# Second attention of a two-block network: the rounding and the rest of q one round later, the output projection cut into three groups of tiles, the output weights rounded later

## The chip, the core and the metric

The kernel runs on one core of one Trainium2 chip. The metric is the device time of one execution in microseconds (us), as the median of several runs. Before the change three runs took 1021.14, 1026.47 and 1027.76 us.

## What is computed

Two transformer blocks on x of shape (2, 512, 512), each one an attention and a feed-forward part with adaptive layer norm. The change touches only the attention of the second block, a latent attention with 32 heads:

```python
q = (rmsnorm(h @ w_qa) @ w_qb)            # per head: 128 plain + 64 rotary
k_c, k_rope = split(h @ w_kva)            # 64 + 64, k_c normalized
k_nope, v = split(k_c @ w_kvb)            # per head
scores = q_head @ k_head.T * 192 ** -0.5
attn = softmax(scores)
out = concat_heads(attn @ v) @ w_o
x = x + ga * out
```

The kernel has folded the key and value weights of each head into the q weights and the output weights before this stage starts. What is left per head is a q of 128 rows (64 latent, 64 rotary), its scores against one shared key, a softmax, a context of 64 latent columns, and an output projection. All matrix products are done in a rounded format with a correction: an operand f is kept as `hi` (rounded, made by ScalarE) and `lo` = f - `hi` (the rest, made by VectorE or GpSimd), and a product is hi*hi + hi*lo + lo*hi.

## The kernel before, in words

**Units, couples, rounds, steps.** A unit u is one head of one batch (64 units). A couple j is two heads (32 couples). Each unit has four rounds, one for each 128 of its 512 query rows, so there are 256 rounds s. All five engines run through the same loop `for s in range(STEPS)`, each with its own list of work for step s; 8 steps are the period of a couple. Below, r stands for s mod 8. Each engine works its own list strictly in the order in which it is written; semaphores tie the lists together.

**The work of one round s.** TensorE: `scores(s)`, three matmuls of 128x128 by 128x512 into one of two PSUM banks (L1289 to L1291), which wait until the exponential of round s-2 has read that bank. VectorE: `row_max(s)` (L1351) reads the scores, then `row_inv(s-1)` (L1358). ScalarE: `exps(s)` (L1429) with the maximum as bias. GpSimd: `normalize(s-1)` (L1488) for three rounds of four, ScalarE for the fourth (L1444). VectorE: `turn(s-3)` (L1366), the 32x32 transposes. When four rounds are turned, 16 DMAs move the unit's blocks (12 on SyncE's queue, 4 on ScalarE's, L1254).

**q of a coming unit.** TensorE projects unit s/4+2 at s mod 4 = 0 (`project`, five matmuls, L1275 to L1279). VectorE turns it by the rotary angles in three operations: part 0 (L1341, in the step with s mod 4 = 1) and parts 1 and 2 (L1343, L1346, s mod 4 = 2). They write `qu` and `qf`, which are parts of the buffer that the profile calls stage_a. GpSimd adds the two, `q_sum` (L1479), at s mod 4 = 3. ScalarE rounds the sum to `q_hi` (`q_round`, L1423) and GpSimd makes `q_lo` (`q_rest`, L1483), both at s mod 4 = 0. There is one `qf` and one `qu`: part 0 of a unit waits for `q_sum` of the unit before it (`ge(dve, qsum, u)`), and part 2 for its `q_lo` (`ge(dve, qlo_done, u)`).

**Context and output projection of couple j.** They run at the steps s = 8(j+2) + r. TensorE: `context` at r = 1 and r = 3, eight matmuls each (L1302). ScalarE: `cT_hi` at r = 3 (L1461). VectorE: `cT_lo` at r = 4 (L1402). The output weights of the couple are rounded by ScalarE to `b_hi` (L1418) and by GpSimd to `b_lo` (L1474), both at r = 0. TensorE: `project_out` of tiles 0 and 1 at r = 5 and tiles 2 and 3 at r = 7, three matmuls a tile (L1316 to L1318), accumulated in four PSUM banks over 16 couples. The weights of a coming couple's q are rounded at r = 5 (`w_hi` L1414, `w_lo` L1469), and once at s = 0.

**The order inside a step** is that of the code. GpSimd's list in a step is: `normalize`, `q_rest`, `weights`, `out_weights`, `q_sum`, where each of them is due. ScalarE's is: `exps`, `q_round`, its share of the normalizing, its DMAs, `weights`, `out_weights`, `cT_hi`. TensorE's is: `scores`, `project`, `context`, `project_out`.

**Ends of a batch.** When the 16 couples of a batch are accumulated, VectorE multiplies the four banks by the gate, adds them to x and takes statistics (`evict`, `stats_of`; L1372, L1376, L148), in step 144 for the first batch and in the last step for the second.

Of the kernel before, what the change touches and what calls it, by code (L numbers as in the profile page):

```python
# [35 lines left out]
HP = NH // 2  # L36
UNITS = 2 * NH
COUPLES = NH
# [36 lines left out]
def megakernel(nc, a, out):  # L75
# [3 lines left out]
    with ExitStack() as whole:  # L79
# [872 lines left out]
        with ExitStack() as ph:  # L952
# [263 lines left out]
            TURN_LAG = 3  # L1216
            MOVE_LAG = TPB + TURN_LAG
            PV_AT = {1: (0, 1), 3: (2, 3)}
            OUT_AT = {5: (0, 1), 7: (2, 3)}
            ROUNDS = TPB * UNITS  # L1220
            STEPS = 8 * (COUPLES + 2) + 1

            def ge(eng, s_, v):
                if v > 0:
                    eng.wait_ge(s_, v)

            def placed(at, s):

                j, r = s // 8 - 2, s % 8
                return (j, at[r]) if r in at and 0 <= j < COUPLES else None  # L1230

            def norm_ready(eng, s):

# [23 lines left out]
            with nc.Block() as block:  # L1257
# [75 lines left out]
                @block.vector  # L1333
                def _(dve):
                    def rotate(u, part):

                        lo, hi = slice(KVR, KVR + 32), slice(KVR + 32, P)
                        if part == 0:
                            dve.wait_ge(q_ps, u + 1)
                            ge(dve, qsum, u)  # L1340
                            dve.tensor_tensor(qu[lo, :], q_bank[hi, :], sinq[hi, :], ALU.mult).then_inc(qrot, 1)  # L1341
                        elif part == 1:
                            dve.tensor_tensor(qu[hi, :], q_bank[lo, :], sinq[lo, :], ALU.mult).then_inc(qrot, 1)  # L1343
                        else:
                            ge(dve, qlo_done, u)
                            dve.tensor_tensor(qf[:, :], q_bank[:, :], cosq[:, :], ALU.mult).then_inc(qrot, 1)  # L1346

                    def row_max(s):
                        dve.wait_ge(s_ps, s + 1)
                        ge(dve, exp_done, s - RING + 1)  # L1350
                        dve.tensor_reduce(nmax[:, s % RING:s % RING + 1], s_bank[s % 2][:, :], AX.X, ALU.max,  # L1351
                                          negate=True).then_inc(max_done, 1)

                    def row_inv(s):
                        dve.wait_ge(exp_done, s + 1)
                        if s >= RING:
                            norm_ready(dve, s - RING)
                        dve.reciprocal(rinv[:, s % RING:s % RING + 1], rsum[:, s % RING:s % RING + 1]).then_inc(rinv_done, 1)  # L1358

                    def turn(s):  # L1360

                        u, st = s // TPB, s % TPB
                        norm_ready(dve, s)
                        if st == 0 and u >= T_SLOTS:
                            pT_ready(dve, u - T_SLOTS)
                        dve.transpose(blk[:, u % T_SLOTS, :, :, 32 * st:32 * st + 32].rearrange("p j k q -> p k j q"),  # L1366
                                      prob[s % RING]).then_inc(blk_done, 1)

                    def evict(b):
                        for n in range(TPB):  # L1370
                            dve.wait_ge(o_ps, 2 * HP * (b + 1) - 1 + n // 2)
                            dve.tensor_tensor(o_bank[n][:, :], o_bank[n][:, :], gate[:, 0, b, :], ALU.mult).then_inc(og_done, 1)  # L1372
                        for n in range(TPB):
                            i = TPB * b + n
                            dve.wait_ge(og_done, i + 1)
                            dve.tensor_tensor(x[:, i, :], o_bank[n][:, :], x[:, i, :], ALU.add).then_inc(x3_done, 1)  # L1376

                    def stats_of(b):
                        for t in range(TPB * b, TPB * (b + 1)):
                            dve.wait_ge(x3_done, t + 1)  # L1380
                            tile_stats(dve, t)

                    dve.wait_ge(acc_set, 1)
                    for u in (0, 1):
                        for part in range(3):
                            rotate(u, part)
                    for s in range(STEPS):
                        if s < ROUNDS:
                            row_max(s)
                        if 1 <= s <= ROUNDS:  # L1390
                            row_inv(s - 1)
                        if s % TPB == 1 and s // TPB + 2 < UNITS:
                            rotate(s // TPB + 2, 0)
                        if s % TPB == 2 and s // TPB + 2 < UNITS:
                            rotate(s // TPB + 2, 1)
                            rotate(s // TPB + 2, 2)
                        if TURN_LAG <= s < ROUNDS + TURN_LAG:
                            turn(s - TURN_LAG)
                        if s % 8 == 4 and 0 <= s // 8 - 2 < COUPLES:
                            j = s // 8 - 2  # L1400
                            dve.wait_ge(chi_done, j + 1)
                            dve.tensor_tensor(by_block(cT_lo[:, :]), ct_bank[:, :].rearrange("p (g t q) -> p g t q", g=QD, t=TPB),  # L1402
                                              by_block(cT_hi[:, :].bitcast(F32)), ALU.subtract).then_inc(clo_done, 1)
                        for b in range(B):
                            if s == 8 * (HP * (b + 1) + 2):
                                evict(b)
                                stats_of(b)

                @block.scalar
                def _(act):  # L1410
# [3 lines left out]
                        act.activation(w_hi[:, :, :, :], wq_all[:, 2 * p:2 * p + 2, :, :], ACT.Copy).then_inc(whi_done, 1)  # L1414

                    def out_weights(j):
                        ge(act, o_ps, 2 * j)
                        act.activation(b_hi[:, :], wb_all[:, j % HP, :], ACT.Copy).then_inc(bhi_done, 1)  # L1418

                    def q_round(u):  # L1420
# [14 lines left out]
                    for s in range(STEPS):  # L1435
                        u, st = s // TPB, s % TPB
                        if s < ROUNDS:
                            exps(s)
                        if st == 0 and u + 1 < UNITS:
                            q_round(u + 1)  # L1440
                        if st == (ACT_NORM + 2) % TPB and 1 <= u <= UNITS:
                            n = s - 2
                            act.wait_ge(rinv_done, n + 1)
                            act.activation(prob[n % RING], prob[n % RING], ACT.Copy,  # L1444
                                           scale=rinv[:, n % RING:n % RING + 1]).then_inc(norm_act, 1)
                        if 0 <= (s - MOVE_LAG) // TPB < UNITS:
                            m, jj = (s - MOVE_LAG) // TPB, (s - MOVE_LAG) % TPB
                            if jj == 0:
                                move_ready(act, m)
                            move(act, m, QD - 1, jj).then_inc(pT_in[m % P_SLOTS], 16)  # L1450
                        if s == 0:
                            weights(1)
                        if s % 8 == 5 and s // 8 + 2 < COUPLES:
                            weights(s // 8 + 2)
                        if s % 8 == 0 and 0 <= s // 8 - 2 < COUPLES:
                            out_weights(s // 8 - 2)
                        if s % 8 == 3 and 0 <= s // 8 - 2 < COUPLES:
                            j = s // 8 - 2
                            act.wait_ge(pv_ps, 2 * (j + 1))
                            ge(act, o_ps, 2 * j)  # L1460
                            act.activation(by_block(cT_hi[:, :]), ct_bank[:, :].rearrange("p (g t q) -> p g t q", g=QD, t=TPB),  # L1461
                                           ACT.Copy).then_inc(chi_done, 1)

                @block.gpsimd
                def _(pool):
# [30 lines left out]
                    for s in range(STEPS):  # L1496
                        u, st = s // TPB, s % TPB
                        if 1 <= s <= ROUNDS and (s - 1) % TPB != ACT_NORM:
                            normalize(s - 1)
                        if st == 0 and u + 1 < UNITS:  # L1500
                            q_rest(u + 1)
                        if s == 0:
                            weights(1)
                        if s % 8 == 5 and s // 8 + 2 < COUPLES:
                            weights(s // 8 + 2)
                        if s % 8 == 0 and 0 <= s // 8 - 2 < COUPLES:
                            out_weights(s // 8 - 2)
                        if st == 3 and u + 2 < UNITS:
                            q_sum(u + 2)
# [186 lines left out]
```

## Time and profile before

| | |
|---|---|
| median of three runs | 1026.47 us |
| the profiled execution, its time | 1023.77 us |
| its span, first to last instruction | 1021.9 us |
| mean granted TensorE clock | 0.934 |
| the stage that the change touches | from 392.1 us (first row maximum) to 952.5 us (last output projection) |

Busy time over the whole span: TensorE 849.0 us (83%), VectorE 764.2 (75%), ScalarE 535.6 (52%), GpSimd 520.7 (51%). A row of the profile gives an instruction's start, its duration, and in square brackets how long its engine had been idle before it and which instruction released it. An instruction's duration reaches into the next one's on VectorE and ScalarE, and much further on TensorE, so the cost of an instruction to its engine is read from the distance between starts.

### The profile page before, as it was taken

How to read it: one execution, taken by the hardware profiler on the slowest of the kernel's cores; microseconds unless marked ns; L12 is line 12 of the kernel's file. 1: busy time of each engine (PE TensorE's matmuls, PEld its weight loads, DVE VectorE, ACT ScalarE, POOL GpSimd, SP SyncE). 2: the span in 40 equal slices, each digit the busy share in tenths (PEclk: the TensorE clock that was granted, in tenths of full speed). 3: DMA queues.
4: the chain of work that ended last, by engine and by line, in shares of the span. 5: the costliest groups of instructions: out<-in, count | busy, mean ns of one | idle time of the engine just before them, and what ended most of it. 6: DMA issues, size and time to landing. Idle time of an engine off the chain costs nothing. (4 is left out here: it accounts for less than half of the span.)

```text
span 1021.9 us, 15116 instructions
## 1 busy us (share of the span) xinstructions
PE 849.0 (83%) x4552; PEld 563.1 (55%) x4552; DVE 764.2 (75%) x1588; ACT 535.6 (52%) x1142; POOL 520.7 (51%) x449
## 2 busy tenths in 40 slices
PE   5678886599978965799999999997999999985476
PEld 1667675477767743355555555564555555643145
DVE  1759998745535525999999999999999999982453
ACT  2267874623213743665666666564666665662143
POOL 2034342012110004888888888886888888872013
PEclk9979998599987986999999999998999999998779
DMA  9430000700023770455555555553555555555101
GB/s 328 159 129 2 1 2 1 276 23 1 1 82 126 246 227 0 111 132 126 130 130 129 128 132 131 126 131 93 129 128 132 128 130 129 127 130 118 56 11 72
DMA packets 73105, 112.29 MB, mean 110 GB/s; under 512 B 18816, under 2 KB 23936, under 8 KB 72768
## 3 DMA queue, kind: packets, MB, share of 16 engines
q1 hardware_dynamic: 60736, 94.54, 33.8%
q10 hardware_dynamic: 12288, 16.79, 6.9%
q8 instruction: 36, 0.59, 0.2%
q14 instruction: 45, 0.37, 0.1%
HBM read 42.06 MB, written 2.10 MB: 43 GB/s over the span
## 5 line engine op out<-in xcount | busy, mean ns | idle before, releaser
L1351 DVE TENSOR_REDUCE nmax<-bank 128x1 f32<-128x512 f32 x256 | 171.7, 671 | 36.1 <-PE bank L1291 35.9
L1429 ACT ACTIVATE prob<-bank,nmax 128x512 f32<-128x512 f32 x172 | 118.2, 687 | 132.9 <-DVE nmax L1351 132.1
L1488 POOL TENSOR_TENSOR prob<-prob,rinv 128x512 f32<-128x512 f32 x129 | 133.5, 1042 | 42.7 <-DVE rinv L1358 42.7
L1289 PE MATMUL bank<-xk_hi,q_hi 128*128 128x512 f32 x256 | 114.2, 446 | 28.0 <-ACT prob L1429 20.8
L1366 DVE STREAM_TRANSPOSE blk<-prob 128x512 f32<-128x512 f32 x172 | 120.0, 698 | 1.7 <-ACT prob L1444 0.4
L1289 PEld LDWEIGHTS bank<-xk_hi,q_hi 128*128 128x128 f32 x256 | 48.2, 188 | 108.8 <-issue 53.0
L1483 POOL TENSOR_TENSOR q_lo<-stage_a,q_hi 128x512 fp32r<-128x512 f32 x64 | 82.6, 1291 | 47.8 <-ACT q_hi L1423 47.8
L1290 PE MATMUL bank<-xk_lo,q_hi 128*128 128x512 f32 x256 | 101.5, 396 | 0.0
L1291 PE MATMUL bank<-xk_hi,q_lo 128*128 128x512 f32 x256 | 100.9, 394 | 0.0
L1429 ACT ACTIVATE stage_a<-bank,nmax 128x512 f32<-128x512 f32 x84 | 57.7, 687 | 56.4 <-DVE nmax L1351 56.0
L1479 POOL TENSOR_TENSOR stage_a<-stage_a 128x512 f32<-128x512 f32 x64 | 82.0, 1282 | 6.3 <-DVE stage_a L1346 6.3
L204 ACT ACTIVATE n_f<-bank,mod 128x128 f32<-128x128 f32 x128 | 48.2, 463 | 50.4 <-PE bank L195 49.2
L1316 PE MATMUL bank<-b_hi,cT_hi 128*128 128x512 f32 x128 | 54.0, 422 | 22.2 <-DVE cT_lo L1402 22.2
L1488 POOL TENSOR_TENSOR stage_a<-stage_a,rinv 128x512 f32<-128x512 f32 x63 | 65.2, 1041 | 13.6 <-DVE rinv L1358 13.6
L1302 PE MATMUL bank<-raw_e,c_all 128*64 128x512 f32 x256 | 63.2, 617 | 5.5 <-DMA raw_e<-blk 5.5
L1302 PE MATMUL bank<-pT,c_all 128*64 128x512 f32 x256 | 64.2, 625 | 3.6 <-DMA pT<-blk 3.6
L1366 DVE STREAM_TRANSPOSE blk<-stage_a 128x512 f32<-128x512 f32 x84 | 58.6, 697 | 0.6
L794 POOL TENSOR_TENSOR f_g<-f_sum,gate 128x512 f32<-128x512 f32 x8 | 10.2, 1271 | 95.4 <-DVE f_sum L870 95.4
L1423 ACT ACTIVATE q_hi<-stage_a 128x512 fp32r<-128x512 f32 x64 | 40.4, 631 | 31.4 <-POOL stage_a L1479 31.4
L1341 DVE TENSOR_TENSOR stage_a<-bank,stage_a 32x512 f32<-32x512 f32 x64 | 44.5, 695 | 14.4 <-PE bank L1279 12.3
L1291 PEld LDWEIGHTS bank<-xk_hi,q_lo 128*128 128x128 f32 x256 | 48.5, 190 | 11.3
L214 DVE TENSOR_TENSOR n_h_lo<-n_f,n_h_hi 128x512 fp32r<-128x512 f32 x24 | 16.6, 692 | 46.8 <-ACT n_h_hi L210 46.8
(217 smaller groups left out, 2135.6 us busy)
## 6 DMA issues: line engine op xcount, KB each, us to landing
pT<-blk SPq DMA_DIRECT2D x384, 64.0 KB, 2.0
raw_e<-blk SPq DMA_DIRECT2D x384, 64.0 KB, 2.0
wmod<-in_wmod SPq DMA_DIRECT2D x12, 1024.0 KB, 12.0
raw_e<-in_wo SPq DMA_DIRECT2D x8, 1024.0 KB, 6.4
pT<-blk ACTq DMA_DIRECT2D x128, 64.0 KB, 2.1
raw_e<-blk ACTq DMA_DIRECT2D x128, 64.0 KB, 2.0
wqn<-in_wqn SPq DMA_DIRECT2D x8, 512.0 KB, 4.0
stage_a<-in_wqkv SPq DMA_DIRECT2D x4, 768.0 KB, 8.9
```

Of the source, the lines that this page charges most:

```text
L204: a_ = act.activation(self.f[:, c, :], pT[:, c * P:(c + 1) * P], ACT.Identity, bias=mod3[:, self.shift + c, b:b + 1], scale=mod3[:, self.s ...
L1289: pe.matmul(sbk, q_hi[:, u % 2, q], xk_hi[:, 2, ks], start=True, stop=False)
L1290: pe.matmul(sbk, q_hi[:, u % 2, q], xk_lo[:, 1, ks], start=False, stop=False)
L1291: pe.matmul(sbk, q_lo[:, u % 2, q], xk_hi[:, 2, ks], start=False, stop=True).then_inc(s_ps, 1)
L1302: mm = pe.matmul(ct_bank[e * KVR:(e + 1) * KVR, :], c_all[:, b * TPB + kt, :], pT[(2 * j + e) % P_SLOTS][:, :, kt * P:(kt + 1) * P], start ...
L1316: pe.matmul(o_bank[n][:, :], cT_hi[:, ts], b_hi[:, :], start=(p == 0), stop=False)
L1351: dve.tensor_reduce(nmax[:, s % RING:s % RING + 1], s_bank[s % 2][:, :], AX.X, ALU.max, negate=True).then_inc(max_done, 1)
L1366: dve.transpose(blk[:, u % T_SLOTS, :, :, 32 * st:32 * st + 32].rearrange("p j k q -> p k j q"), prob[s % RING]).then_inc(blk_done, 1)
L1429: act.activation(prob[s % RING], s_bank[s % 2][:, :], ACT.Exp, bias=nmax[:, s % RING:s % RING + 1], accum_out=rsum[:, s % RING:s % RING + ...
L1479: pool.tensor_tensor(qf[:, :], qf[:, :], qu[:, :], ALU.add).then_inc(qsum, 1)
L1483: pool.tensor_tensor(q_lo[:, u % 2, :], qf[:, :], q_hi[:, u % 2, :].bitcast(F32), ALU.subtract).then_inc(qlo_done, 1)
L1488: pool.tensor_tensor(prob[s % RING], prob[s % RING], bc(rinv[:, s % RING:s % RING + 1], [P, S]), ALU.mult).then_inc(norm_pool, 1)
```

## The change

- `q_round` on ScalarE and `q_rest` on GpSimd move from the step with s mod 4 = 0 to the step with s mod 4 = 1, behind the exponential (ScalarE) or the normalizing (GpSimd) of that step.
- `project_out` is called three times a couple in place of twice: tiles 0 and 1 at r = 6, tile 2 at r = 7, and tile 3 at r = 10, which is r = 2 of the next couple's period. The semaphore `o_ps` therefore counts 3 a couple, and the waits on it are changed to match.
- `out_weights` on both engines moves from r = 0 to r = 3. On ScalarE it stands ahead of `cT_hi`, on GpSimd ahead of `q_sum`.
- `evict` and the statistics of a batch move three steps later, and the loop has four steps more.
- `placed` is rewritten so that it can look past the end of a period.

```diff
-            OUT_AT = {5: (0, 1), 7: (2, 3)}
+            OUT_AT = {6: (0, 1), 7: (2,), 10: (3,)}
-            STEPS = 8 * (COUPLES + 2) + 1
+            STEPS = 8 * (COUPLES + 2) + 5
             def placed(at, s):
-                j, r = s // 8 - 2, s % 8
-                return (j, at[r]) if r in at and 0 <= j < COUPLES else None
+                for r, parts in at.items():
+                    j = (s - r) // 8 - 2
+                    if (s - r) % 8 == 0 and 0 <= j < COUPLES:
+                        return j, parts
+                return None
                     def evict(b):
                         for n in range(TPB):
-                            dve.wait_ge(o_ps, 2 * HP * (b + 1) - 1 + n // 2)
+                            dve.wait_ge(o_ps, 3 * HP * (b + 1) - 2 + max(n - 1, 0))
...
-                            if s == 8 * (HP * (b + 1) + 2):
+                            if s == 8 * (HP * (b + 1) + 2) + 3:
                                 evict(b)
...
# ScalarE
                     def out_weights(j):
-                        ge(act, o_ps, 2 * j)
+                        ge(act, o_ps, 3 * j)
...
-                        if st == 0 and u + 1 < UNITS:
+                        if st == 1 and u + 1 < UNITS:
                             q_round(u + 1)
...
-                        if s % 8 == 0 and 0 <= s // 8 - 2 < COUPLES:
+                        if s % 8 == 3 and 0 <= s // 8 - 2 < COUPLES:
                             out_weights(s // 8 - 2)
                         if s % 8 == 3 and 0 <= s // 8 - 2 < COUPLES:
                             j = s // 8 - 2
                             act.wait_ge(pv_ps, 2 * (j + 1))
-                            ge(act, o_ps, 2 * j)
+                            ge(act, o_ps, 3 * j)
...
# GpSimd
-                        if st == 0 and u + 1 < UNITS:
+                        if st == 1 and u + 1 < UNITS:
                             q_rest(u + 1)
...
-                        if s % 8 == 0 and 0 <= s // 8 - 2 < COUPLES:
+                        if s % 8 == 3 and 0 <= s // 8 - 2 < COUPLES:
                             out_weights(s // 8 - 2)
                         if st == 3 and u + 2 < UNITS:
                             q_sum(u + 2)
```

## Rows read from the trace of the kernel before

**Rows 1.** Windows: stretch, length, busy of PE, PEld, DVE, ACT, POOL; clock; DMA

```profile
520.00:610.00 90.00, 84.05 (x341) 51.50 (x343) 84.09 (x172) 55.54 (x125) 74.81 (x67) 1.00 0.56 130
```

**Rows 2.** Waits, 400 to 940 us: who for whom, total, times, longest

```profile
DVE nmax L1351 <- PE bank L1291: 35.5, 62, 7.5
```

**Rows 3.** VectorE's timeline over one couple, from r = 2 on

```profile
718.09 0.69 DVE L1351 TENSOR_REDUCE nmax<-bank 128x1 f32<-128x512 f32 x1 [0.53 <-PE bank L1291]
...
720.84 0.65 DVE L1351 TENSOR_REDUCE nmax<-bank 128x1 f32<-128x512 f32 x1
...
723.34 0.65 DVE L1402 TENSOR_TENSOR cT_lo<-bank,cT_hi 128x512 fp32r<-128x512 f32 x1
723.91 0.67 DVE L1351 TENSOR_REDUCE nmax<-bank 128x1 f32<-128x512 f32 x1
...
724.68 0.69 DVE L1341 TENSOR_TENSOR stage_a<-bank,stage_a 32x512 f32<-32x512 f32 x1
...
726.42 0.69 DVE L1351 TENSOR_REDUCE nmax<-bank 128x1 f32<-128x512 f32 x1 [0.29 <-PE bank L1291]
...
729.16 0.65 DVE L1351 TENSOR_REDUCE nmax<-bank 128x1 f32<-128x512 f32 x1
...
731.68 0.69 DVE L1351 TENSOR_REDUCE nmax<-bank 128x1 f32<-128x512 f32 x1
```

**Rows 4.** ScalarE and GpSimd in the same couple, r = 3 to 5

```profile
721.52 0.69 ACT L1429 ACTIVATE stage_a<-bank,nmax 128x512 f32<-128x512 f32 x1 [1.93 <-DVE nmax L1351]
722.20 0.60 ACT L1461 ACTIVATE cT_hi<-bank 128x512 fp32r<-128x512 f32 x1
722.63 1.28 POOL L1479 TENSOR_TENSOR stage_a<-stage_a 128x512 f32<-128x512 f32 x1
723.95 0.63 ACT L1423 ACTIVATE q_hi<-stage_a 128x512 fp32r<-128x512 f32 x1 [0.40 <-POOL stage_a L1479]
...
724.66 1.30 POOL L1483 TENSOR_TENSOR q_lo<-stage_a,q_hi 128x512 fp32r<-128x512 f32 x1 [0.74 <-ACT q_hi L1423]
```

**Rows 5.** b_hi and b_lo, and the normalizing behind them

```profile
716.51 0.63 ACT L1418 ACTIVATE b_hi<-wb_all 128x512 fp32r<-128x512 f32 x1
...
717.88 1.28 POOL L1474 TENSOR_TENSOR b_lo<-wb_all,b_hi 128x512 fp32r<-128x512 f32 x1
719.12 2.04 POOL L1488 TENSOR_TENSOR prob<-prob,rinv 128x512 f32<-128x512 f32 x2
```

**Rows 6.** TensorE's timeline: output projection and scores at r = 5 and 6

```profile
724.04 0.50 PE L1316 MATMUL bank<-b_hi,cT_hi 128*128 128x512 f32 x1 [0.62 <-DVE cT_lo L1402]
...
725.99 0.39 PE L1291 MATMUL bank<-xk_hi,q_lo 128*128 128x512 f32 x1
```

**Rows 7.** From the maximum of r = 7 to that of r = 2

```profile
729.85 0.69 ACT L1429 ACTIVATE prob<-bank,nmax 128x512 f32<-128x512 f32 x1 [1.93 <-DVE nmax L1351]
730.68 0.50 PE L1289 MATMUL bank<-xk_hi,q_hi 128*128 128x512 f32 x1 [0.40 <-ACT prob L1429]
731.57 1.94 PE L1302 MATMUL bank<-pT,c_all 128*64 128x512 f32 x8
...
734.44 0.69 DVE L1351 TENSOR_REDUCE nmax<-bank 128x1 f32<-128x512 f32 x1 [0.53 <-PE bank L1291]
```

**Rows 8.** The stage's start: weights, and what waits for them

```profile
394.17 1.27 POOL L1483 TENSOR_TENSOR q_lo<-stage_a,q_hi 128x512 fp32r<-128x512 f32 x1 [1.12 <-ACT q_hi L1423]
395.39 1.26 POOL L1469 TENSOR_TENSOR w_lo<-wq_all,w_hi 128x512 fp32r<-128x512 f32 x1
396.70 0.79 PE L1275 MATMUL bank<-xk_hi,w_hi 128*128 128x512 f32 x1 [4.67 <-POOL w_lo L1469]
```

**Rows 9.** VectorE around the end of the first batch (s = 144 and 145)

```profile
690.61 0.65 DVE L1351 TENSOR_REDUCE nmax<-bank 128x1 f32<-128x512 f32 x1
...
698.99 0.68 DVE L1351 TENSOR_REDUCE nmax<-bank 128x1 f32<-128x512 f32 x1
```

**Rows 10.** The stage's last context

```profile
942.92 5.10 PE L1302 MATMUL bank<-raw_e,c_all 128*64 128x512 f32 x16 [5.54 <-DMA raw_e<-blk]
```

## The prediction, made blind

> **What bounds the kernel now.** I read the windows first, to see which engine is full in the stretch that the change touches. VectorE is busy for 84.09 of 90 us there and the clock is at its full 1.00 [rows 1]. TensorE's 84.05 is a sum of overlapping records; by distances between starts, eight context matmuls take 1.87 us (start to the scores behind them), 0.23 each, and a couple's 62 matmuls (24 scores, 10 of q, 16 context, 12 output) some 14.5 us. So the pace is VectorE's, and the list of waits says what it still waits for: TensorE's scores, 62 times, 35.5 us [rows 2]. VectorE's timeline over a couple shows where. A couple takes 16.35 us (718.09 to 734.44, r = 2 to r = 2), and 62 waits over some thirty couples are two a couple: 0.53 us at r = 2, 0.29 at r = 6 [rows 3, 7]. All else is its own work, 15.5 us. A change that alters neither the work nor these waits moves nothing; the most to be won is 0.8 us a couple.
>
> The wait at r = 6. TensorE's output projection stands ahead of `scores` of r = 6 and waits for `cT_lo`; it starts at 724.04, and the last score matmul starts at 725.99, 0.43 us before the maximum [rows 3, 6]. The exponential on which those scores also depend had started at 722.77 (`cT_hi` at 722.20 plus 0.57) and was no obstacle.
>
> The wait at r = 2. It hangs on a chain that starts at VectorE itself: maximum of r = 7 at 729.16, exponential 729.85, scores of r = 1 730.68, eight context matmuls 731.57, scores of r = 2, maximum 734.44: 5.28 us, of which VectorE could have done its own steps in 4.75 [rows 3, 7].
>
> **The output projection in three parts.** No matmul is added. With tiles 0 and 1 behind the scores of r = 6, these no longer wait for `cT_lo`, and the 0.29 us go. Tiles 0 and 1 then fill the time in which scores of r = 7 wait for their exponential anyway. Tile 3 (three matmuls, 0.7 us) now lies between the scores of r = 2 and r = 3. The scores of r = 2 are ahead of it, so the wait of 0.53 stays. Behind it the scores of r = 4 come later, by at most 0.7 us. The earlier exponential of r = 1 (next part) gives part of that back, and I put what is left at 0 to 0.16 us at r = 4, which is no term of its own, for the chain below starts at r = 3 and passes it by.
>
> **q one round later.** At r = 1 and r = 5 the exponential is no longer queued behind `q_hi`. But VectorE paces ScalarE; an earlier exponential is worth something only if TensorE was waiting on it in front of a late score, which is so neither at r = 2 nor at r = 6. `q_lo` comes later: its readers are part 2 of the rotation and the scores of the next unit. With `q_hi` 0.68 behind the exponential and `q_lo` 0.71 behind that [rows 4], `q_lo` is done 3.4 us behind the step's maximum, and part 2 is reached 3.7 us behind it at the earliest (the step's 2.25 without its wait, and 1.5). Zero, with a cover of 0.3; where it is gone, VectorE waits for the difference.
>
> **The output weights later: the step that decides.** `b_hi` on ScalarE now stands behind the exponential of r = 3 and ahead of `cT_hi`; `b_lo` on GpSimd stands ahead of `q_sum`. Queued behind `b_lo` is `q_sum`, and for `q_sum` waits VectorE's part 0 at r = 5, which overwrites `qu`. Count from the maximum of r = 3 (720.84). Now: exponential at +0.68, `cT_hi` +1.36, `q_sum` +1.79 to +3.07, `cT_lo` +2.50, maximum of r = 5 +3.07, part 0 +3.84, maximum of r = 6 +5.58 [rows 3, 4]. After: `b_hi` takes the place of `cT_hi` at +1.36. `b_lo` starts 0.71 later as `q_lo` does behind `q_hi` [rows 4], at +2.07. The next GpSimd instruction starts 1.24 to 1.27 behind it [rows 5]: `q_sum` at +3.33, done at +4.61. Part 0 can start at about +4.65, where it was ready at +3.84: a new wait of 0.8 us. From part 0 to the next maximum are 726.42 - 0.29 - 724.68 = 1.45 us, so the maximum of r = 6 is at +6.10 in place of +5.58: **0.52 us more a couple**, with the old wait at r = 6 already taken off. `cT_hi` comes 0.6 later, `cT_lo` could start at +2.56 instead of +2.50, and that lies inside the new wait. So does the 0.16 of tile 3.
>
> No row of before has VectorE waiting for `q_sum` here, so the handover is bounded: 0.04 us as ScalarE's (722.63 + 1.28 to 723.95) [rows 4] up to 0.1. The five terms are each good to 0.02. I take 0.52 and keep 0.42 to 0.6.
>
> At r = 7 nothing is put ahead of `q_sum`. GpSimd's list is refilled there by `w_lo` and two normalizings that come 1.3 us later than now, and by my count it has 0.5 us to spare before the value that it needs at r = 7.
>
> **How often.** `b_lo` with a part 0 two steps behind it occurs at s = 19, 27, ... 243: 29 times. Once, at s = 147, the batch's end covers it. 28 x 0.52 = 14.6 us (28 x 0.42 = 11.8).
>
> **Once each.** The batch's end costs 7.1 us of VectorE's own work (690.61 to 698.99, less a step of 1.25) [rows 9]. At r = 0 it hid the wait of r = 2 and left the 0.29 of r = 6; at r = 3 it hides the new one of r = 5 and leaves the 0.53 of r = 2: +0.2. Start: `w_lo` at s = 0 no longer stands behind a `q_lo` (394.17 to 395.39), and the projection that TensorE waits 4.67 us for starts 1.2 us sooner [rows 8]; the `q_lo` that is pushed back is then wanted by part 2 two steps on, so I take -1.0. End: tile 3 of couple 30 falls between the halves of the last context, which had waited 5.54 us for its DMA [rows 10]: 0.7 us more, up to 1.4 at half the clock; +1.0. The DMAs: SyncE's queue and ScalarE's four are moved past nothing that they wait for. Sum: 14.6 + 0.2 - 1.0 + 1.0 = **+14.8 us**, on the profiled execution's 1023.77: 1038.6. The median is 2.7 above that execution and would give 1041.3; the three runs spread over 6.6, so I stay by the profiled one and say 1039.
>
> **A rule against the change.** The granted clock is 1.00 in this stage although the matmuls come in groups with gaps [rows 1]. The Trainium skill (TensorE: Matmul & The Clock Gate, "A second HAM failure mode: psum-queue depth-cycling") tells of a kernel in which small idle times between groups of matmuls made the clock swing between its two levels. The gap that the new wait makes on TensorE is under 1.5 us, no more than now. If the clock did fall to 1.2 GHz, 62 matmuls would take 29 us in place of 14.5, some 12.7 us over the present 16.35 a couple; one couple in four would be +90 us. By that rule the kernel would be slower by that; I give it 0.02.
>
> **The rivals.**
> - *The hidden one, on the faster side.* The wait for scores at r = 6 goes and `q_sum` is in time: -0.29 x 28 - 1.0 = -9.1 us, 1014.7 on the profiled execution. It is decided at one point: `q_sum` must end before VectorE is ready for part 0, +3.84. That needs 0.8 us off a chain of exponential, `b_hi`, `b_lo` and `q_sum`, each of which has a row. Against it speaks all of rows 4 and 5; for it only that GpSimd's order may not bind as I read it. 0.06.
> - *The trade.* `q_sum` is late, but part is given back (a wait at r = 2 that shrinks, a shorter end): -3 to +8, say +4, 1028. For it: both are waits of one engine on another. Against it: the chain of r = 2 starts at VectorE's own maximum and moves along. 0.15.
> - *Two waits.* Tile 3 on TensorE or the late `w_lo` on GpSimd pushes a second reader, the maximum of r = 4 or part 0 at r = 1, 0.3 to 0.5 us more a couple: +23 to +28, 1049. For it: covers of 0.2 to 0.5 us. 0.12.
>
> **How the numbers follow.** Forecast 0.65, trade 0.15, two waits 0.12, hidden 0.06, clock 0.02. The range 1027 to 1049 takes in the forecast with 0.42 to 0.6, the upper half of the trade and the lower half of the two waits. About 1%, 10 us, is what runs of this kernel can tell from no change. Slower by over 1%: 0.14 and most of the forecast, 0.57, 0.71. Within 1%: the trade, 0.08 of the forecast and most of the hidden one, 0.25. Faster by over 1%: 0.04.
>
> **What would show it.** VectorE waits 0.7 to 0.8 us for GpSimd's `q_sum` ahead of part 0 at r = 5, 28 times; the waits for scores fall from 62 to about 31 and keep 0.53 each; a couple takes 16.9 us; `b_lo` follows `b_hi` at once, with `q_sum` right behind. I am wrong if part 0 at r = 5 has no wait, if a couple takes under 16.3 us or over 17.3, or if the clock leaves 1.00.

## The result, and the profile after

The changed kernel takes 1042.80 us (median of 4 runs, 1041.84 to 1045.10), beside 1025.62 for the kernel before (4 runs): a ratio of 1.0177, 95% interval 1.0138 to 1.0216. It is **slower by 1.8%**, 17 us. The forecast was 1039, range 1027 to 1049, and slower by over 1% with a chance of 0.71. The profiled execution took 1041.84 us with a span of 1040.0, clock 0.932; the one before had 1023.77, 1021.9 and 0.934.

The list of waits from 400 to 960 us, read as in [rows 2]:

```profile
DVE nmax L1354 <- PE bank L1294: 21.1, 35, 1.4
DVE stage_a L1344 <- POOL stage_a L1482: 20.2, 28, 1.0
POOL b_lo L1477 <- ACT b_hi L1421: 15.6, 31, 8.6
```

The waits for scores fell from 62 to 35, and their 35.5 us to 21.1. The two totals are not quite alike: that of before holds one wait of 7.5 us at the stage's start (ended at 400.25), and its counterpart of 6.5 us ended at 397.03, ahead of this window. Without it, 61 waits of 28.0 us became 35 of 21.1. In the place of those that went, VectorE waits 28 times, 20.2 us, 0.72 each, for `q_sum`: a line that the list of before does not have. The timeline shows where, from the maximum of r = 3 to that of r = 6, the rows that answer to [rows 3, 4]:

```profile
781.32 0.65 DVE L1354 TENSOR_REDUCE nmax<-bank 128x1 f32<-128x512 f32 x1
782.68 0.62 ACT L1421 ACTIVATE b_hi<-wb_all 128x512 fp32r<-128x512 f32 x1
782.72 0.69 DVE L1354 TENSOR_REDUCE nmax<-bank 128x1 f32<-128x512 f32 x1
783.38 1.30 POOL L1477 TENSOR_TENSOR b_lo<-wb_all,b_hi 128x512 fp32r<-128x512 f32 x1 [0.22 <-ACT b_hi L1421]
784.59 0.67 DVE L1354 TENSOR_REDUCE nmax<-bank 128x1 f32<-128x512 f32 x1
784.62 1.30 POOL L1482 TENSOR_TENSOR stage_a<-stage_a 128x512 f32<-128x512 f32 x1
786.03 0.70 DVE L1344 TENSOR_TENSOR stage_a<-bank,stage_a 32x512 f32<-32x512 f32 x1 [0.70 <-POOL stage_a L1482]
787.50 0.69 DVE L1354 TENSOR_REDUCE nmax<-bank 128x1 f32<-128x512 f32 x1
```

`b_hi` starts 1.36 us behind the maximum of r = 3, `b_lo` 2.06, `q_sum` 3.30, part 0 of the rotation 4.71, the maximum of r = 6 6.18. That last distance was 5.58 to 5.61. The couple takes 16.95 us in place of 16.38.

VectorE is less busy than in [rows 1] (81.42 us in place of 84.09), and the clock is the same in this stretch:

```profile
520.00:610.00 90.00, 82.94 (x333) 49.67 (x332) 81.42 (x165) 53.95 (x126) 73.61 (x65) 1.00 0.54 126
```

Two places outside the steady couples. At the start of the stage, `q_lo` of unit 1 now comes late, part 2 of the rotation and the scores of round 4 wait for it, and TensorE's clock falls:

```profile
400.44 0.69 DVE L1349 TENSOR_TENSOR stage_a<-bank,stage_a 128x512 f32<-128x512 f32 x1 [0.28 <-POOL q_lo L1486]
400.46 0.51 PE L1292 MATMUL bank<-xk_hi,q_hi 128*128 128x512 f32 x1 [0.91 <-POOL q_lo L1486]
...
401.62 0.63 PE L1278 MATMUL bank<-xk_hi,w_hi 128*128 128x512 f32 x1
402.04 0.63 PE L1279 MATMUL bank<-xk_lo,w_hi 128*128 128x512 f32 x1
...
404.88 0.69 DVE L1354 TENSOR_REDUCE nmax<-bank 128x1 f32<-128x512 f32 x1 [1.22 <-PE bank L1294]
```

From 401.62 to 402.04 are 0.42 us between two matmuls, nearly twice the 0.23 of the steady stage: the granted clock was 0.74 over 398 to 404 us, against 0.85 before. From 400.8 to 404.2 us it was 0.50, the lower of the two levels, and again from 424.7 to 428.1, where the kernel before had 1.00 from 399.8 us on. At the end, tile 3 stands between the halves of the last context, as [rows 10] did not have it:

```profile
960.06 3.18 PE L1305 MATMUL bank<-raw_e,c_all 128*64 128x512 f32 x8 [4.35 <-DMA raw_e<-blk]
963.17 0.80 PE L1319 MATMUL bank<-b_hi,cT_hi 128*128 128x512 f32 x1
963.76 0.52 PE L1320 MATMUL bank<-b_lo,cT_hi 128*128 128x512 f32 x1
964.12 0.40 PE L1321 MATMUL bank<-b_hi,cT_lo 128*128 128x512 f32 x1
964.45 1.94 PE L1305 MATMUL bank<-raw_e,c_all 128*64 128x512 f32 x8
```

### The profile page after: what moved, and what is told of

The parts are those of the page before. It is cut to its first block and busy times, and to the rows that moved or that the text cites. A ratio compares the mean times of both kernels' runs of the same rounds, so it can differ in the third digit from the quotient of the medians.

```text
span 1040.0 us, 15116 instructions
## 1 busy us (share of the span) xinstructions
PE 856.4 (82%) x4552; PEld 563.1 (54%) x4552; DVE 767.4 (74%) x1588; ACT 527.7 (51%) x1142; POOL 523.3 (50%) x449
## 5 line engine op out<-in xcount | busy, mean ns | idle before, releaser
L1292 PE MATMUL bank<-xk_hi,q_hi 128*128 128x512 f32 x256 | 118.3, 462 | 59.5 <-ACT prob L1432 34.0
L1344 DVE TENSOR_TENSOR stage_a<-bank,stage_a 32x512 f32<-32x512 f32 x64 | 44.5, 696 | 33.8 <-POOL stage_a L1482 20.2
L1477 POOL TENSOR_TENSOR b_lo<-wb_all,b_hi 128x512 fp32r<-128x512 f32 x32 | 41.3, 1290 | 29.1 <-ACT b_hi L1421 29.1
L1293 PEld LDWEIGHTS bank<-xk_lo,q_hi 128*128 128x128 f32 x256 | 49.3, 192 | 4.3
```

The lines of the kernel that those rows point to most:

```text
L1292: pe.matmul(sbk, q_hi[:, u % 2, q], xk_hi[:, 2, ks], start=True, stop=False)
L1293: pe.matmul(sbk, q_hi[:, u % 2, q], xk_lo[:, 1, ks], start=False, stop=False)
```

## The experiments

Each ratio is to the kernel before, run on the same chip beside it. "Mean couple" is the distance between the maxima of r = 0 at s = 32 and s = 136 in the profiled execution, divided by 13; "shortest" is the shortest couple among these. Before: 16.38 and 16.36; changed: 16.98 and 16.94.

| kernel | median us | ratio (95%) | mean couple | shortest |
|---|---|---|---|---|
| changed, `q_sum` ahead of `b_lo` | 1031.84 | 1.0039 (1.0020 to 1.0058) | 16.61 | 16.27 |
| before, output weights later | 1042.65 | 1.0139 (1.0103 to 1.0174) | 16.96 | 16.92 |
| before, output projection at 6 and 7 | 1026.25 | 0.9983 (0.9957 to 1.0010) | 16.53 | 16.09 |
| before, q later | 1027.19 | 1.0007 (0.9984 to 1.0030) | 16.45 | 16.44 |
| changed, tile 3 back at r = 7 | 1041.84 | 1.0154 (1.0130 to 1.0179) | 16.97 | 16.93 |
| changed, output weights at r = 2 | 1034.28 | 1.0087 (1.0057 to 1.0118) | 16.74 | 16.29 |
| projection 6/7, 2 moves to ScalarE | 1024.87 | 0.9980 (0.9960 to 1.0000) | 16.36 | 16.29 |
| projection 6/7, context in 3 | 1019.92 | 0.9943 (0.9912 to 0.9973) | 16.14 | 15.93 |
| the same, 2 moves to ScalarE | 1024.36 | 0.9974 (0.9954 to 0.9993) | 16.62 | 16.28 |
| context in 3, q later, weights at r = 2 | 1029.21 | 1.0031 (1.0001 to 1.0060) | 16.42 | 15.93 |
| the same, 2 moves to ScalarE | 1013.24 | 0.9860 (0.9822 to 0.9898) | 15.98 | 15.93 |
| the same, 1 move to ScalarE | 1010.62 | 0.9858 (0.9814 to 0.9902) | 15.95 | 15.93 |

The medians of different rows were partly taken on different chips; the kernel before, run beside them, had 1026.24 us (rows 1 to 4), 1026.49 (rows 5 and 7 to 9) and 1027.02 (rows 6 and 10 to 12).

### Which of the three parts costs

**The changed kernel with the order of two calls on GpSimd turned round.**

```diff
-                        if s % 8 == 3 and 0 <= s // 8 - 2 < COUPLES:
-                            out_weights(s // 8 - 2)
                         if st == 3 and u + 2 < UNITS:
                             q_sum(u + 2)
+                        if s % 8 == 3 and 0 <= s // 8 - 2 < COUPLES:
+                            out_weights(s // 8 - 2)
```

> The changed kernel with one edit: on GpSimd, q_sum stands ahead of out_weights at r = 3. Theory (the queue order on GpSimd is the loss): VectorE's wait for q_sum at r = 5 (0.70 us, 28 times) disappears, part 0 follows the reciprocal at once; the couple falls from 16.95 to 16.35-16.4 us (5.58 + 0.15 of tile 3 from the maximum of r = 3 to that of r = 6, less the old 0.29), about 16 us less than the changed kernel: 1026 us, no different from the kernel before. Rival (tile 3 between the scores, or the later q, costs the time): the couple stays at 16.9 and the time at 1042.

The wait for `q_sum` is gone from the list, as expected, the step of r = 5 is 2.24 us in place of 2.91, and the shortest couple is 16.27, just under the 16.35 expected. The time is not: 1031.8 and not 1026, so 11 of the 17 us came back. Between s = 32 and s = 136 every second couple took 17.0. The list of waits from 440 to 900 us says why:

```profile
PE bank L1305 <- DMA pT<-blk: 6.5, 10, 0.7
```

The context at r = 1 waits for the moved blocks, ten times, 0.65 us each. In the same stretch neither the kernel before nor the changed one has such a line.

**The kernel before with the output weights later, and nothing else.**

```diff
-                        if s % 8 == 0 and 0 <= s // 8 - 2 < COUPLES:
+                        if s % 8 == 3 and 0 <= s // 8 - 2 < COUPLES:
                             out_weights(s // 8 - 2)
```

(on both engines)

> The kernel before with only out_weights moved from r = 0 to r = 3 on ScalarE and GpSimd; output projection still at r = 5 and 7. Theory: the whole loss comes from this step, so VectorE waits for q_sum at r = 5, about 0.8 us, and the 0.29 us at r = 6 is covered by it; couple 16.9 us, +0.5 x 28 = +15 us: 1040. A second wait could stand behind it: the output projection at r = 5 now waits for b_lo, done 3.4 us behind the maximum of r = 3, and the scores of r = 6 stand behind it; by the count they are ready at +5.3, before +6.1. Rival (the step is harmless alone): couple 16.4, 1026.

1042.65, mean couple 16.96: this step alone brings the whole loss, within the noise. The waits from 400 to 960 us:

```profile
DVE stage_a L1341 <- POOL stage_a L1479: 23.4, 28, 1.2
PE bank L1316 <- POOL b_lo L1474: 27.3, 28, 1.2
```

The second wait that I had named (the projection at r = 5 for `b_lo`) is there too, 28 times, and costs VectorE nothing, since it ends first.

**The kernel before with the projection of tiles 0 and 1 at r = 6.**

```diff
-            OUT_AT = {5: (0, 1), 7: (2, 3)}
+            OUT_AT = {6: (0, 1), 7: (2, 3)}
```

> The kernel before with only the output projection's first half moved from r = 5 to r = 6 (tiles 0, 1 at r = 6, tiles 2, 3 at r = 7). Theory: the wait at r = 6 for scores (0.29 us a couple) goes and no other comes: couple 16.1 us, 30 x -0.28 = -8 us, 1017. The wait of 0.53 at r = 2 stays. Rival (the wait moves on to r = 7 or r = 0, since six more matmuls stand between the scores of r = 6 and those of r = 7 and r = 0): couple 16.4, 1026.

The part on r = 6 holds, the result does not. The step of r = 5 to 6 fell from 2.53 to 2.24 us and the shortest couple to 16.09. But the mean couple rose to 16.53, above that of before. In the step of r = 1 to 2 some couples are longer by 0.7, 1.3 or 2.9 us. At one of them:

```profile
528.41 1.94 PE L1302 MATMUL bank<-pT,c_all 128*64 128x512 f32 x8 [1.23 <-DMA pT<-blk]
```

And SyncE's queue in the same stretch, first issue of a couple's 24, time until the last is issued, number:

```profile
509.40 17.49 SPq L1254 DMA_DIRECT2D pT<-blk  x24
526.99 15.79 SPq L1254 DMA_DIRECT2D raw_e<-blk  x24
```

The next couple's 24 begin at 542.88, then 559.61, 575.77, 593.36: one group behind the other with 0.1 us between them, 16.8 us each on the mean. That is longer than VectorE's 16.1. VectorE was not what the queue waited for: at the six group starts from 509.40 to 593.36 its last transpose had ended 0.6 to 2.1 us before the queue came free. The couple that was longer by 2.9 us (from 592.34) had a wait for blocks of 1.21 us like others, and behind it the clock was at its lower level, 0.51 over 595 to 598.5 us:

```profile
594.78 3.47 PE L1302 MATMUL bank<-pT,c_all 128*64 128x512 f32 x8 [1.21 <-DMA pT<-blk]
```

The same eight matmuls took 1.94 us at 528.41. In the changed kernel the queue has room:

```profile
544.93 16.57 SPq L1257 DMA_DIRECT2D pT<-blk  x24
561.88 15.94 SPq L1257 DMA_DIRECT2D raw_e<-blk  x24
```

with 16.95 from start to start. So a new theory: **SyncE's queue is a second floor**, about at the pace of the kernel before.

**The kernel before with q later.**

```diff
-                        if st == 0 and u + 1 < UNITS:
+                        if st == 1 and u + 1 < UNITS:
```

(on both engines)

> The kernel before with only q_round and q_rest one round later. Theory: at r = 1 q_lo now stands behind b_lo and a normalizing on GpSimd, so that part 2 of the rotation at r = 2 waits for it by 0.1 to 0.3 us: couple 16.5, +3 to +8 us, 1030. At the start of the stage the first projection comes 1 us sooner, but q_lo of unit 1 is late for the scores of round 4: +0.6 together. Rival A (free, cover of 0.3 holds): 1026. Rival B (an earlier exponential at r = 1 and 5 is worth something): couple under 16.3, 1023 or less.

1027.19, ratio 1.0007: no measurable difference, where I had expected +3 to +8 us. Of the wait at part 2 only 0.07 us a couple showed (the step of r = 2 to 3 takes 2.82 in place of 2.75), so rival A is the one that came. Nothing speaks for an earlier exponential being worth something by itself. The stage's start is that of the changed kernel: the first eight rounds take 21.33 us (changed: 21.34; before: 20.75), with the clock at 0.50 from 401.6 to 405.0. That loss belongs to the later q.

**The changed kernel with tile 3 back at r = 7**

```diff
-            OUT_AT = {6: (0, 1), 7: (2,), 10: (3,)}
+            OUT_AT = {6: (0, 1), 7: (2, 3)}
```

(with the waits on `o_ps` as before)

> The changed kernel with the third group undone: tiles 2 and 3 both at r = 7, nothing at r = 10; q later and output weights at r = 3 stay. Theory (GpSimd's order is the loss, the third group costs only ends): VectorE still waits for q_sum at r = 5, now 0.8 us, since the maximum of r = 4 is no longer 0.15 late; couple still 16.9; the end of the stage is 1 to 2 us shorter: 1041. Rival (the third group costs the time): couple 16.4, 1027.

1041.84 and a mean couple of 16.97: the third group costs next to nothing in the steady stage. The step of r = 3 falls from 1.40 back to 1.25, and the wait for `q_sum` takes it all back (3.05 in place of 2.91 at r = 5), since both hang on the maximum of r = 3. From the last maximum to the end of the statistics it takes 35.9 us in place of 36.8.

**The changed kernel with the output weights at r = 2** (`s % 8 == 2` in place of `s % 8 == 3`, on both engines).

> The changed kernel with out_weights at r = 2 in place of r = 3 on both engines; q later and the output projection in three groups stay. Theory (only b_lo's place directly ahead of q_sum costs): b_lo ends some 2.7 us before part 0 of r = 5 wants q_sum, the wait of 0.70 us goes, couple 16.3 in VectorE's own pace; but SyncE's queue then holds every second couple at 17.0, as in the run with q_sum ahead: mean 16.65, 1030. Rival: the wait stays, 1042.

1034.28. The wait for `q_sum` is gone (step of r = 5: 2.24), the shortest couple is 16.29, and the queue again holds couples back: seven waits for moved blocks from 440 to 900 us, mean couple 16.74. That is 0.09 above the expectation, and the median 4 us. One of these couples took 19.28 us: its wait of 1.2 us was followed by a stretch at the lower clock (661.1 to 664.5 us), as in the run with the projection at 6 and 7.

### The second floor

**Projection at r = 6 and 7, two of twelve moves given to ScalarE.**

```diff
# SyncE
                             for jj in range(QD):
+                                if g == QD - 2 and jj % 2:
+                                    continue
                                 move(sp, u, g, jj).then_inc(pT_in[u % P_SLOTS], 16)
# ScalarE
                             move(act, m, QD - 1, jj).then_inc(pT_in[m % P_SLOTS], 16)
+                            if jj % 2:
+                                move(act, m, QD - 2, jj).then_inc(pT_in[m % P_SLOTS], 16)
```

> The kernel before with the output projection at r = 6 and 7, and 2 of SyncE's 12 moves of a unit given to ScalarE's queue (10 and 6 in place of 12 and 4). Theory B (SyncE's queue took the gain back): every couple takes 16.1, no context waits for its DMA, 30 x -0.28 = -8 us, and the end, where 24 moves run one behind the other, is 2 to 3 us shorter: 1015. Theory A (the queue was not in the way; the stretched couples have another cause): 1026 as without it. Bound: a second issue of 0.5 us on ScalarE in steps r = 0, 2, 4, 6 may delay an exponential by up to 0.5.

The waits for moved blocks are gone in the stage and the end is 3.2 us shorter (31.65 in place of 34.84), about as expected. But the couple is 16.3 and not 16.1, and the time 1024.9 and not 1015. The bound that I had named fits: ScalarE's second issue at r = 0 stands ahead of `b_hi`,

```profile
ACT b_hi L1420 <- issue: 19.2, 28, 1.9
```

and behind it, by the order of the lists, are the exponential of r = 1, the scores of r = 3, a context and the scores of r = 4. The step of r = 3 took 1.42 us in place of 1.25. So this run neither proved nor refuted the queue as the floor.

**Projection at r = 6 and 7, and the context in three parts.**

```diff
-            PV_AT = {1: (0, 1), 3: (2, 3)}
+            PV_AT = {1: (0,), 2: (1,), 3: (2, 3)}
```

(with three counts of `pv_ps` a couple)

> The kernel before with the output projection at r = 6 and 7, as in the second run on record here, and the context cut in three: tile 0 at r = 1, tile 1 at r = 2, tiles 2 and 3 at r = 3. This takes away both waits of VectorE for scores. Theory A (VectorE's own work is the only floor): couple 15.6 to 15.8, -18 us, 1008. Theory B (SyncE's queue is a second floor: its 24 DMA issues a couple took 15.9 to 17.5 us, back to back, in the run with the projection at r = 6 and 7): the mean couple stays at 16.4 to 16.7, the last context of a couple waits for its DMA, and the time stays at 1020 to 1027.

1019.92: the wait at r = 2 is gone too (2.26 in place of 2.76), which confirms the chain of [rows 7]. It comes out at the edge of what theory B said, and the mean couple of 16.14 is below it: the queue kept up with 16.14 here, less than the 16.38 of before. Six waits for moved blocks are left, and a step of r = 3 of 1.63 us in place of 1.25. I put that down to an exponential of r = 1 that stands behind `q_hi` and `b_hi`; the runs below speak against it.

**The same with two moves given to ScalarE.**

> The context in three parts, the output projection at r = 6 and 7, and 2 of SyncE's 12 moves of a unit given to ScalarE's queue. Theory B: with the queue out of the way (20 issues of 0.66 us are 13.3 us a couple) VectorE's own work sets the pace: couple 15.6 to 15.8, -0.7 x 30 = -20 us, the end 2 to 3 us shorter: 1004. Theory A expects the same time as for the run without the moved DMAs, 1008. If ScalarE's second issue delays exponentials: 16.1, 1015.

1024.36, slower than without: a miss for theory B as I had put it, and its last sentence, on delayed exponentials, names what came, at a higher price. The step of r = 2 rose by 0.3 us in the median and 0.6 on the mean, and from 440 to 900 us VectorE waited 25 times, 10.0 us, for exponentials ahead of `row_inv`, where the run without the moved DMAs has no such line. ScalarE's list was now the obstacle (SyncE's queue stood idle 3.2 us a couple), so the pair says nothing on SyncE's.

**Context in three, projection at r = 6 and 7, q later, output weights at r = 2.** This clears ScalarE's list at r = 0.

> The context in three parts and the output projection at r = 6 and 7, with the changed kernel's later q and the output weights at r = 2. In the context run the step from r = 3 to 4 took 1.63 us instead of 1.25, because the exponential of r = 1 stood behind q_hi and b_hi. Theory: with both out of its way that step is 1.25 and VectorE's pace is 15.6; SyncE's queue (15.4 to 17.1 us a couple in that run) then holds the mean at 15.9 to 16.1: 1017 to 1020. If the queue were no floor: 1010.

1029.21, outside what I expected: VectorE's shortest couple is 15.93, but thirteen contexts wait for moved blocks and the mean is 16.42. The step of r = 3 did not come down to 1.25 either: it is 1.55 in the couples without such a wait and 1.9 in those with one. From 440 to 900 us:

```profile
PE bank L1302 <- DMA pT<-blk: 12.4, 13, 1.3
```

**The same with one move in twelve given to ScalarE** (`jj == 3` in place of `jj % 2`), **and with two.**

> As the kernel beside it, with 1 move of 12 given to ScalarE (11 and 5), in the step with s mod 4 = 2 alone. SyncE's 22 issues are then some 14.6 to 15.4 us a couple, just below VectorE's 15.6: couple 15.7, the end 1.5 us shorter, 1008. If the second issue hurts: less than with two moved, 1012.

> The kernel of the run beside it with 2 of SyncE's 12 moves of a unit given to ScalarE (10 and 6). Theory (SyncE's queue is the second floor, and ScalarE's second issue hurt before only where q_hi and b_hi stood behind it at r = 0): couple 15.7, no DMA waits, the end 3 us shorter: 1007. If the second issue on ScalarE delays exponentials in any case: couple 16.2, 1018.

1010.62 and 1013.24. One DMA of sixteen issued from another queue takes the time from 1029.2 to 1010.6, with nothing else altered. With one moved, every couple from s = 16 on takes 15.93 to 15.97 us, but for the one with the batch's end (with two moved, one of 16.50 and one of 16.27 are left). SyncE's queue now has room, 0.68 us behind the first group shown:

```profile
521.23 15.20 SPq L1254 DMA_DIRECT2D raw_e<-blk  x22
537.09 15.94 SPq L1254 DMA_DIRECT2D pT<-blk  x22
```

With one moved, what is left of waits for moved blocks from 440 to 900 us is

```profile
PE bank L1291 <- DMA pT<-blk: 1.2, 3, 0.4
PE bank L1291 <- DMA raw_e<-blk: 0.4, 1, 0.4
```

(here the release is seen at the next matmul). VectorE is busy for 86.92 of 90 us where it had 84.09:

```profile
520.00:610.00 90.00, 87.67 (x349) 49.52 (x349) 86.92 (x176) 55.93 (x129) 77.30 (x69) 1.00 0.57 133
```

The pair shows the second floor: it lies in SyncE's queue. Both kernels beat the one before, by 1.4%. The couple of 15.95 is still above my 15.7, because the step of r = 3 takes 1.55 in place of 1.25. The trace shows what holds those scores, and it is TensorE's own work:

```profile
554.47 0.50 PE L1291 MATMUL bank<-xk_hi,q_hi 128*128 128x512 f32 x1 [0.39 <-ACT prob L1431]
...
559.16 1.94 PE L1304 MATMUL bank<-pT,c_all 128*64 128x512 f32 x8
561.03 0.50 PE L1291 MATMUL bank<-xk_hi,q_hi 128*128 128x512 f32 x1
...
562.03 0.69 DVE L1353 TENSOR_REDUCE nmax<-bank 128x1 f32<-128x512 f32 x1 [0.22 <-PE bank L1293]
```

From the scores of r = 1 (554.47) to those of r = 4 (561.03) TensorE's timeline shows no wait: three rounds of scores and the sixteen context matmuls take 6.56 us, and VectorE's own steps over the same three rounds 6.26 (2.26, 2.75 and 1.25). So in these rounds TensorE is a third floor, 0.3 us above VectorE's.

## Why the prediction was right

**The step that decides** held to a tenth of a microsecond, and the mechanism was the forecast one. `b_lo` was due at +2.07 and came at +2.06, `q_sum` +3.33 and +3.30, part 0 +4.65 and +4.71, the maximum of r = 6 +6.10 and +6.18. The handover from `q_sum` to VectorE was 0.11 us (785.92 to 786.03), a little above the 0.04 to 0.1 that I had allowed. The wait is 0.72 and not 0.8, because tile 3 makes the maximum of r = 4 late by 0.15, within my 0 to 0.16; without tile 3 the wait was 0.83 (the runs with tile 3 back at r = 7, and with the output weights alone). Turning the two calls on GpSimd round took the wait away, and moving the output weights alone onto the kernel before brought the loss: the cause is shown from both sides. That turning them round gave back 11 us and not 17 is the second floor's doing.

**The term for a couple** was 0.52, measured 0.57. Times 28 that is 16.0 in place of 14.6. Four couples (s from 16, 120, 152 and 160) had 0.3 to 0.6 more, 1.8 together. The one from s = 16 (426.2 us) starts inside the stretch at the lower clock that ended at 428.1; with tile 3 back at r = 7 and no such stretch it took 17.59 and not 18.19. The other three are not explained. The batch's end was +0.2, measured +0.44; behind it the clock was 0.50 for 10.3 us (711.4 to 721.7), before for 6.8 (696.7 to 703.5), and what that is worth is not separated.

**The start** was taken at -1.0 and was +0.6. The 0.95 came, between the first two maxima. But I saw only one reader of the late `q_lo`, part 2 of the rotation (0.28), and not the scores of round 4, and not that TensorE's clock could fall there: another 1.3 us together. The clock fell to its lower level in this place in seven of the eight profiled kernels with the later q, the changed one among them, and in none of the six without it. In the eighth (context in three, q later, no move given away) the scores of round 4 had waited the same 0.91 us, the clock stayed up until 411.7 us, and the first eight rounds took 20.06 us, 0.7 less than before: nearly the forecast gain. So the 1.3 us are the price of the clock, and the gap by itself does not settle whether it is paid.

**The end** was taken at +1.0, with +1.4 at half the clock. From the last maximum on it is 2.0 us longer, but the seven steps ahead of that maximum ran 0.4 shorter, so that 1.6 is left. Of it 1.2 lies between the last context's start and the projection behind it (6.5 before, 7.75 after); tile 3's three matmuls take 1.28 us there (963.17 to 964.45), where the clock came up from its lower level at 964.0.

**Sum.** 17.8 + 0.4 + 0.6 in the loop, 0.4 less in its last steps, 2.0 at the end: 20.4, against 14.8 forecast. The terms were too small by 3.2 for the couples (28 of them at 0.57, and the four longer ones), 0.2 for the batch's end, 1.6 for the start and 0.6 for the end. The span grew by only 18.1, because the work ahead of the stage, which the change does not touch, ran 2.3 us shorter in this execution; that the total came nearer to the forecast by this is luck. By the medians it is 17.2.

**The rivals.** The hidden one is excluded by the wait for `q_sum`. The trade is excluded too: the wait of r = 2 kept its 0.53 us, and the end grew longer. Of the two waits no second one shows in the steady couples. In these the clock stayed at 1.00 (440 to 700 us). Outside them it did leave 1.00, which I had named as a sign of being wrong: twice near the start, behind the first batch's end, and several times from 943.5 us on. The kernel before has low stretches behind the batch's end and in the stage's end as well (from 928.8 us), so "its full 1.00" in the prediction holds for the steady couples and not for the whole stage.

**What was wrong without harm:** "the most to be won is 0.8 us a couple", and that SyncE's queue and ScalarE's four moves were no matter because they "are moved past nothing that they wait for". I had priced only VectorE's floor. Had the two calls on GpSimd stood the other way round, my count would have given a couple of about 16.3 and a time no slower than before, and the chip gave 1031.8: the waits for scores that the change was to remove were worth next to nothing as long as SyncE's queue needed as long as they did. Rows that I did not read would have told. In the kernel before:

```profile
525.88 15.64 SPq L1254 DMA_DIRECT2D raw_e<-blk  x24
542.08 15.82 SPq L1254 DMA_DIRECT2D pT<-blk  x24
```

The queue is idle for 0.56 us between these two groups, and for 0.1 to 0.6 between others.

## What to carry to other kernels

When a step moves to another place in an engine's list, look at what it is now put in front of, and at who waits for that: here an operation of 1.3 us whose own result nobody was waiting for cost 16 us, because a sum stood behind it. Where several engines are near their limit, write down a floor for each of them, the queue of a DMA-issuing engine included (number of issues times the distance between two), before pricing the removal of a wait: the gain ends at the second floor. Removing the waits alone brought nothing (1026.25) or 0.6% (1019.92); with one DMA in sixteen moved to another queue as well, and ScalarE's list cleared for it, 1.4%. Moving DMAs where the other engine's list was full brought nothing (1024.87) or lost part of the gain (1024.36).

## What the runs showed of the hardware

- From one issue of a 64 KB move to the next on SyncE's queue it was 0.63 us in the median and 0.67 to 0.70 on the mean, nine in ten between 0.58 and 0.88; a group of 24 took 15.4 to 17.5 us. One issue in many groups, always the fifth to seventh, took 1.2 to 2.4 us. It stands only in the groups that write `pT`, which are every second couple's (10 of 12 of them in the kernel before, none of those that write `raw_e`), and nearly all contexts that waited for blocks are in those couples. Its cause stays open.
- The full queue is the limit that the Trainium skill lists second in "What "DMA-bound" means" (Perfetto Trace Analysis): the issuing engine's track filled with DMA issues from end to end. The trace of the kernel with the projection at 6 and 7 agrees: 0.10 us between groups, with the 16 DMA engines busy for a mean share of only 0.54. Whether the time goes into the issuing or into something behind it on the same queue, no run here separates.
- The Trainium skill (DMA: Bandwidth & Descriptors, "Issuing engines are not separate DMA queues") says that starting DMAs from several engines saves only the sequencer's time, which is usually small beside the DMA. Here it was not small: 0.63 us in the median against 2.0 from issue to landing, and one DMA in sixteen issued elsewhere was worth 18.6 us.
- The queue's floor is no fixed number. In the kernels that it holds back the mean couple was 16.14 to 16.74 us with the same 24 issues, and the kernel before ran at 16.38 with no wait for moved blocks from 440 to 900 us. No run here tells apart a slower issue and a missed chance to catch up.
- In three kernels one wait of 1.2 to 1.3 us for blocks was followed by a stretch at the lower clock (0.51 over 595 to 598.5 us in one of them), and that couple took 1.6 to 1.7 us more than couples with the same wait that kept 1.00 (19.02 against 17.39, 19.28 against 17.58, 18.82 against 17.23). What decides between the two stays open.
